# Attention over channels: the eight queries with the most keys move to ScalarE as one exponential per query and head, and TensorE sums them over the keys

## The chip, the cores and the metric

One core of one Trainium2 chip runs the whole program. The metric is device time in microseconds (us) of one execution. The five engines run in parallel, each with its own in-order instruction queue, and meet only at semaphores: TensorE (PE; its weight loads are shown as PEld), VectorE (DVE), ScalarE (ACT), GpSimd (POOL) and SyncE (SP), which issues DMAs.

## The reference, cut to what matters

The program is one transformer-like layer: a state-space recurrence, a mixture of experts, a combine step, and last an attention with a feed-forward part. The change touches the last part alone. There the attention is taken inside each token: with 16 heads of 64 channels, every channel of q is a query and every channel of k a key.

```
Q = (x @ Wq + bq).reshape(b, s, 16, 64) * 64 ** -0.5     # K, V alike, without the factor
scores = einsum("bshq,bshk->bshqk", Q, K)                # an outer product: q[i] * k[j]
scores = where(j > i, -inf, scores)                      # query i sees keys 0..i
w = softmax(scores)
attn = einsum("bshqk,bshk->bshq", w, V)
out = x + attn.reshape(b, s, 1024) @ Wo + bo + (silu(x @ Wg) * (x @ Wu)) @ Wd
```

For one token and head that is 64 x 65 / 2 = 2,080 products, exponentials and weighted values. Query 63 has 64 keys, query 0 has one.

## The kernel before, in words

4,096 tokens are cut into 32 tiles of 128, one token to a partition, and the tiles are run one after the other by one loop. Channels are kept in reverse order with the 16 heads innermost, so a query is a stretch of 16 elements. The queries are split in two units of 32: unit 0 is channels 31 to 0, unit 1 is channels 63 to 32. A tile is 24 chunks: chunks 0 to 7 are unit 0 against the near keys (31 to 0), chunks 8 to 15 are unit 1 against the near keys, a full rectangle, and chunks 16 to 23 are unit 1 against the far keys (63 to 32). The two triangles are cut by diagonals, four to a chunk; a chunk of the rectangle is four keys against all 32 queries. The chunks are 256 to 2,048 elements wide, 34,816 a tile.

Each chunk goes through five steps on four engines.

- DVE `products` (L1238, L1239 in the helper `multiply`): q times k, into one of six slots `s`. It waits until the slot's user six chunks before has been summed and multiplied.
- POOL (L1303): subtracts the maximum `m` of each query and head. The maximum is the greater of q times the largest and q times the smallest key that the query sees; POOL makes it in three instructions of 512 elements for each unit (`maxima`, L1283, L1285, L1288) from two scans of DVE.
- ACT (L1389): the exponential, with the factor 1/8 as a constant scale.
- PE `sum_den` and DVE `times_v`: PE adds the rows of the chunk into the PSUM bank `den`, by one transposing matmul against the identity for each 128 columns (`sum_rows`, L1550); DVE multiplies the chunk by v into one of four slots `pv`.
- PE `sum_num`: the same transposing sum of `pv` into the bank `num`.

Every engine's queue is written out by hand per chunk: at chunk c, PE does `sum_den(c)`, then `prepare(c)`, then `sum_num(c - 1)`, then a part of `down`. `prepare` makes the projections of K and Q for the next tile, V, and the feed-forward up-projections. They all use one PSUM bank, `work`: each fills it only after ACT has copied the one before out of it (`keep_k`, `keep_q`, `keep_v`, `keep_up`), and the tables such as `KEEP_Q0 = 19` or `SILU = 18` say after which chunk's exponential ACT does which copy. `show_k` and `show_v` put a unit's k or v into the PSUM banks `kp` and `vp` that DVE reads. DVE runs `times_v` three chunks behind `products`.

Of the kernel before, what the change touches and what calls it, by code (L numbers as in the profile page):

```python
# [1123 lines left out]
ROWS = 4  # L1124
FRONT = (ROWS - 1) * H
QL = FRONT + HALF
FULL, TAIL = ROWS * HALF, 64
LEAST = 65
HU = H // 2
NTRI = 2 * NB  # L1130
TRI_ORDER = ((0, 7, 2, 5, 4, 3, 6, 1), (0, 1, 2, 3, 4, 7, 6, 5))
NCH = 3 * NTRI
S_RING, PV_RING = 6, 4
NUP = HT // 2
USES = {"U0": 1, "K0": 2, "K1": 3, "V1": 4, "U1": 5, "U2": 6, "Q0": 7, "V0": 8, "Q1": 9}
# [6 lines left out]
def attention_and_ffn(nc, k, io, scratch):  # L1142
    with ExitStack() as ctx:
# [6 lines left out]
        q = [a.sb(f"q{i}", [P, QL]) for i in range(2)]  # L1150
        m = [a.sb(f"m{i}", [P, QL]) for i in range(2)]
        k_near, vv, fall = (a.sb(s, [P, HALF]) for s in ("k_near", "v", "fall"))
        k_far = [a.sb(f"k_far{u}", [P, HALF]) for u in range(2)]
# [8 lines left out]
        out_sb = a.sb("out_sb", [P, D])  # L1162
# [6 lines left out]
        x2_in, y_out, padded = (a.sem(s) for s in ("x2_in", "y_out", "padded"))  # L1169
        xT_in = [a.sem(f"xT_in{u}") for u in range(2)]  # L1170
# [24 lines left out]
        def work_use(t, name):  # L1195

            return t * NWORK + (5 + USES[name])

        def is_rect(c):
            return NTRI <= c < 2 * NTRI  # L1200
# [4 lines left out]
        def triangle(c):  # L1205

            start = TRI_ORDER[unit_of(c)][c % NTRI] * ROWS
            return start, (RANGE - start) * H
# [4 lines left out]
        def part(ring, c):  # L1213

            n = HALF if is_rect(c) else triangle(c)[1]
            return view(slot(ring, c)[:], [[n, ROWS], [1, n]], FULL - ROWS * n)

        def by_row(ap):

            return bass.AP(tensor=ap.tensor, offset=ap.offset, ap=[ap.ap[0], ap.ap[1], [H, RANGE], [1, H]])  # L1220

        def by_query(x, c):

            if is_rect(c):
                return view(x, [[0, ROWS], [1, HALF]], FRONT)
            return view(x, [[-H, ROWS], [1, triangle(c)[1]]], FRONT)

        def by_key(x, c):

            if is_rect(c):  # L1230
                return view(x, [[H, ROWS], [0, RANGE], [1, H]], (c - NTRI) * ROWS * H)
            start, n = triangle(c)
            return view(x, [[0, ROWS], [1, n]], start * H)
# [7 lines left out]
        with nc.Block() as block:  # L1241

            @block.sync
            def _(sp):
# [8 lines left out]
                def finish(t):  # L1253
                    wait(sp, y_ready, t)
                    settle(sp, settled)
                    sp.dma_start(x2[:], tokens(scratch["x2"])[:, bass.ds(t, 1), :].rearrange("p o d -> p (o d)")
                                 ).then_inc(x2_in, 16)
                    sp.wait_ge(y_ready, t + 1)
                    settle(sp, settled)
                    sp.dma_start(tokens(io["out"])[:, bass.ds(t, 1), :].rearrange("p o d -> p (o d)"), out_sb[:]  # L1260
                                 ).then_inc(y_out, 16)
# [12 lines left out]
            def _(pool):  # L1274
                def maxima(t, h, step):

                    n = t * 2 + h
                    turned = lambda x: view(x[:], [[-1, RANGE], [C, H]], h * RANGE + RANGE - 1)
                    rows = lambda x, at=0: view(x[:], [[H, RANGE], [1, H]], at)
# [6 lines left out]
                    else:  # L1286
                        pool.wait_ge(max_step, n * 3 + 2)
                        nc.gpsimd.tensor_tensor(m[h][:, FRONT:QL], m[h][:, FRONT:QL], fall[:], ALU.subtract  # L1288
                                                ).then_inc(max_step, 1)
# [5 lines left out]
                MAXIMA_HERE, MAXIMA_NEXT = {3: 0, 4: 1, 5: 2}, {21: 0, 22: 1, 23: 2}  # L1295
                GATED = 20

                def tile(t, u):
                    for c in range(NCH):
# [9 lines left out]
                        if c == GATED:  # L1309
                            gated(t)  # L1310

                for h in range(2):
# [4 lines left out]
                for step in range(3):  # L1317
                    maxima(0, 0, step)
                pool.wait_ge(padded, 4)
# [3 lines left out]
            def _(act):  # L1323
                def keep_k(t, u, half, source=work):
# [3 lines left out]
                    for low, dst in ((0, k_near), (RANGE, k_far[u])):  # L1328
                        ins = nc.scalar.copy(view(dst[:], [[H, RANGE], [1, HU]], half * HU),
# [3 lines left out]
                def keep_q(t, h, use, source=work):  # L1333
# [3 lines left out]
                    past = (t - 1) * NCH + (NCH if h else NTRI)  # L1337
                    wait(act, mult_done, past)
                    nc.scalar.copy(q[h][:, FRONT:QL], source[:])
                    wait(act, sub_done, past)  # L1340
                    nc.scalar.activation(m[h][:, FRONT:QL], source[:], ACT.Relu)
                    wait(act, max_step, n * 3)
                    nc.scalar.activation(fall[:], source[:], ACT.Relu, scale=-1.0).then_inc(q_out, 1)
# [11 lines left out]
                def show_k(t, u, h):  # L1355
                    act.wait_ge(k_out, t * 2 + 2)
                    wait(act, mult_done, t * NCH + h * 2 * NTRI)
                    nc.scalar.copy(kp[:], (k_far[u] if h else k_near)[:]).then_inc(kp_ready, 1)

                def show_v(t, h):  # L1360
                    act.wait_ge(v_out, t * 2 + (h + 1))
                    wait(act, pv_done, t * NCH + h * 2 * NTRI)
# [18 lines left out]
                KEEP_Q1, KEEP_V1, KEEP_Q0, KEEP_V0 = 0, 13, 19, 22  # L1381
                SUMS_PAST, SUMS_HERE = 2, 14
                KEEP_UP, SILU = {4: 0, 15: 1, 17: 2}, 18
                KEEP_K = {8: 0, 12: 1}

                def tile(t, u):
                    for c in range(NCH):
# [5 lines left out]
                        if c == KEEP_Q1:  # L1393
                            keep_q(t, 1, t * NWORK + 5)
# [13 lines left out]
                        if c == KEEP_Q0:  # L1408
                            keep_q(t + 1, 0, work_use(t, "Q0"))
                        if c == KEEP_V0:  # L1410
# [10 lines left out]
                keep_v(0, 4, source=first_v)  # L1421
                show_k(0, 0, 0)
# [4 lines left out]
            def _(dve):  # L1427
                v = nc.vector

                def products(t, c):  # L1430
# [3 lines left out]
                    if c in (0, 2 * NTRI):  # L1434
                        dve.wait_ge(kp_ready, t * 2 + (1 + c // (2 * NTRI)))
# [4 lines left out]
                def times_v(t, c):  # L1440
                    dve.wait_ge(exp_done, count(t, c))
                    if c in (0, 2 * NTRI):
                        dve.wait_ge(vp_ready, t * 2 + (1 + c // (2 * NTRI)))
# [34 lines left out]
                def output(t):  # L1478
                    dve.wait_ge(acc_done, t + 1)
                    dve.wait_ge(x2_in, 16 * (t + 1))  # L1480
                    wait(dve, y_out, 16 * t)
                    v.tensor_tensor(out_sb[:], misc[:, 0:D], x2[:], ALU.add).then_inc(y_ready, 1)

                SCAN = {8: (0, 0), 9: (0, 1), 12: (1, 0), 13: (1, 1)}
                DIVIDE_PAST, DIVIDE_HERE = {5: 0, 6: 1, 7: 2}, {20: 0, 21: 1, 22: 2}
# [3 lines left out]
                def tile(t, u):  # L1489
                    for c in range(NCH):  # L1490
# [6 lines left out]
                        elif not first(t):  # L1497
                            times_v(t - 1, NCH + c - LAG)
                        if c in SCAN:
# [21 lines left out]
            def _(pe):  # L1521
                def project(t, u, which, half, into=work):

                    pe.wait_ge(xT_in[u], 8 * (t - u) + 16)
                    cols = slice(half * HALF, half * HALF + HALF)
                    for c in range(DC):
                        nc.tensor.matmul(into[:], xT[u][:, c, :], wqkv[which][:, c, cols], start=(c == 0), stop=False)  # L1527
                    nc.tensor.matmul(into[:], part_rows[:], bias[:, which, cols], start=False, stop=True
# [13 lines left out]
                def sum_rows(dst, ring, c):  # L1542

                    buf, n = slot(ring, c), HALF if is_rect(c) else triangle(c)[1]
                    for x in range(ROWS):
                        late = 0 if is_rect(c) else x * H
                        for b in range(math.ceil((n - late) / P)):
                            at = FULL - (ROWS - x) * n + late + b * P
                            wide = max(LEAST, min(P, n - late - b * P))
                            ins = nc.tensor.matmul(dst[0:wide, b * P:(b + 1) * P], buf[:, at:at + wide], k.ident[:],  # L1550
                                                   start=(c in (0, NTRI) and x == 0 and b == 0), stop=False,
                                                   is_transpose=True, skip_group_check=True)
                    return ins

# [32 lines left out]
                DOWN_HERE, DOWN_PAST = {20: 0, 21: 1, 22: 2, 23: 3}, {2: 4, 5: 5, 8: 6}  # L1587
# [160 lines left out]
```

## Time and profile before

| | |
|---|---|
| median of 2 runs | 3773.43 us (3771.79 to 3775.06) |
| profiled execution | 3769.08 us |
| its span, first to last instruction | 3767.3 us |
| mean granted TensorE clock | 0.973 of full speed |
| busy over the span | PE 93%, POOL 88%, DVE 86%, PEld 81%, ACT 48% |
| attention tiles | from about 914 us to the end |
| chain that ended last | POOL 30%, issue 23%, PE 15%, DVE 6%, ACT 1% |
| costliest group | POOL L1303, 768 instructions, 2506.5 us |

The busy shares are averages over a program of several stages. In the last three quarters of the span the page's slices are all alike: that is the loop over the 32 tiles. "Issue" in the chain is time in which an engine waited for nothing that the profile shows.

### The profile page before, as it was taken

The numbers are of one execution on the slowest core, as the hardware profiler recorded it, in microseconds if no ns is written. First come the engines' busy times: TensorE is split into PE (matmuls) and PEld (weight loads), VectorE is DVE, ScalarE is ACT, GpSimd is POOL, SyncE is SP. The second block draws the span as 40 slices with busy tenths as digits, with TensorE's granted clock in tenths as the row PEclk, the third lists the DMA queues.
The fourth block names the chain that finished last, engine by engine and source line by source line (L and its number), as shares of the span: only waits on it lengthen the run. The fifth ranks groups of instructions, "written<-read, shape, count | busy, mean of one in ns | idle before, by whom it ended". The sixth has DMA issues, their size and how long they took to land.

```text
span 3767.3 us, 72478 instructions
## 1 busy us (share of the span) xinstructions
PE 3493.9 (93%) x25868; PEld 3070.0 (81%) x26061; DVE 3233.5 (86%) x3516; ACT 1808.7 (48%) x2391; POOL 3307.3 (88%) x1507
## 2 busy tenths in 40 slices
PE   3684999977999999999999999999999999999999
PEld 2342988866888888888888888888888888888888
DVE  8422777666999999999999999999999999999998
ACT  1110443444555555555555555555555555555554
POOL 1677555524999999999999999999999999999998
PEclk7797999998999999999999999999999999999999
DMA  9523566684000000000000000000000000000000
GB/s 377 180 102 110 179 205 204 211 315 165 4 5 5 5 7 5 5 8 5 5 6 6 5 5 5 5 5 5 5 5 6 7 5 8 5 5 6 5 5 5
DMA packets 110620, 209.17 MB, mean 56 GB/s; under 512 B 16609, under 2 KB 77281, under 8 KB 110305
## 3 DMA queue, kind: packets, MB, share of 16 engines
q1 hardware_dynamic: 84192, 140.90, 11.4%
q0 software_dynamic: 21504, 59.93, 4.3%
q8 instruction: 191, 3.13, 0.3%
q10 hardware_dynamic: 4608, 4.20, 0.3%
q14 instruction: 125, 1.02, 0.1%
HBM read 183.34 MB, written 107.74 MB: 77 GB/s over the span
## 4 chain that ended last, share of the span: by engine, by line
POOL 30%; issue 23%; PE 15%; DVE 6%; ACT 1%; another core or an unknown queue 0%; POOLq 0%; DVEq 0%; ACTq 0%
POOL at_s L1303 26%; PE at_num L1550 6%; PE at_den L1550 5%; DVE at_s L1238 3%; PE at_work L1527 2%; DVE at_pv L1238 2%; POOL at_m L1288 2%; PE at_work L1537 1%; POOL at_fall L1285 1%; POOL at_m L1283 1%; PE at_misc L1576 1%; DVE at_k_low L1457 1%; PE at_misc L1582 1%; DVE at_k_top L1454 0%; DVE at_pv L1239 0%
## 5 line engine op out<-in xcount | busy, mean ns | idle before, releaser
L1303 POOL TENSOR_TENSOR at_s<-at_s,at_m 128x2048 f32<-128x2048 f32 (+7 forms) x768 | 2506.5, 3307 | 5.2 <-POOL at_m L1288 4.7
L1389 ACT ACTIVATE at_s<-at_s 128x2048 f32<-128x2048 f32 (+7 forms) x768 | 1085.7, 1419 | 1085.1 <-POOL at_s L1303 1084.5
L1550 PE MATMUL at_num<-k_ident,at_pv 128*128 128x128 f32 (+2 forms) x9216 | 1135.9, 273 | 64.9 <-DVE at_pv L1238 54.5
L1550 PE MATMUL at_den<-k_ident,at_s 128*128 128x128 f32 (+2 forms) x9216 | 1138.6, 273 | 18.2 <-ACT at_s L1389 15.9
L1550 PEld LDWEIGHTS at_num<-k_ident,at_pv 128*128 128x128 f32 (+2 forms) x9216 | 1025.8, 139 | 150.2 <-DVE at_pv L1238 84.1
L1550 PEld LDWEIGHTS at_den<-k_ident,at_s 128*128 128x128 f32 (+2 forms) x9216 | 1029.8, 139 | 55.8 <-ACT at_s L1389 19.1
L1239 DVE TENSOR_TENSOR at_pv<-at_s,at_vp 128x2048 f32<-128x2048 f32 (+7 forms) x512 | 690.2, 1348 | 121.9 <-PE at_num L1550 63.2
L1239 DVE TENSOR_TENSOR at_s<-at_q,at_kp 128x2048 f32<-128x2048 f32 (+7 forms) x512 | 689.4, 1347 | 27.7 <-PE at_den L1550 24.3
L1238 DVE TENSOR_TENSOR at_pv<-at_s,at_vp 128x2048 f32<-128x2048 f32 x256 | 583.9, 2281 | 0.0
L1238 DVE TENSOR_TENSOR at_s<-at_q,at_kp 128x2048 f32<-128x2048 f32 x256 | 581.2, 2270 | 0.0
L706 POOL DMA_INDIRECT picked<-moe_yo,moe_row x256 | 245.8, 960 | 172.0 <-ACT moe_yo L761 84.0
L1527 PE MATMUL at_work<-k_region,at_xT 128*128 128x512 f32 x776 | 367.6, 596 | 7.2 <-DMA at_xT<-xT 7.2
L142 POOL DMA_INDIRECT slot_x<-e_xn,e_slot x192 | 190.9, 994 | 136.6 <-DMA slot_x<-k_region 75.4
L728 PE MATMUL moe_gu<-moe_xT,c_w 128*128 128x128 f32 x2048 | 278.4, 279 | 5.7 <-DVE moe_xT L850 5.7
L728 PEld LDWEIGHTS moe_gu<-moe_xT,c_w 128*128 128x128 f32 x2048 | 250.3, 193 | 17.3 <-DVE moe_xT L850 13.2
L1527 PEld LDWEIGHTS at_work<-k_region,at_xT 128*128 128x128 f32 x776 | 133.3, 192 | 101.7 <-issue 93.8
L767 ACT ACTIVATE moe_gate<-moe_gu 128x128 f32<-128x128 f32 x256 | 71.1, 278 | 270.7 <-PE moe_gu L728 270.7
L1537 PE MATMUL at_work<-at_xT,k_region 128*128 128x128 f32 x1536 | 187.2, 275 | 0.0
L1537 PEld LDWEIGHTS at_work<-at_xT,k_region 128*128 128x128 f32 x1536 | 179.1, 192 | 0.0
L844 DVE TENSOR_TENSOR moe_hid<-moe_gate,moe_gu 128x128 f32<-128x128 f32 x256 | 73.1, 286 | 104.9 <-ACT moe_gate L767 99.5
L735 PE MATMUL moe_yp<-c_w,moe_hid 128*128 128x256 f32 x512 | 153.3, 381 | 0.3 <-DVE moe_hid L844 0.3
L850 DVE COPY moe_xT<-moe_tr 128x256 f32<-128x256 f32 x256 | 107.1, 418 | 47.3 <-PE moe_tr L719 45.9
(248 smaller groups left out, 3007.0 us busy)
## 6 DMA issues: line engine op xcount, KB each, us to landing
c_w<-experts SPq DMA_DIRECT2D x256, 384.0 KB
slot_x<-k_region SPq DMA_DIRECT2D x16, 2144.0 KB, 25.0
moe_x<-slot_x SPq DMA_DIRECT2D x256, 134.0 KB
cmb_y<-picked SPq DMA_DIRECT2D x32, 768.0 KB, 9.1
at_xT<-xT SPq DMA_DIRECT2D x33, 128.0 KB, 2.0
e_x<-u SPq DMA_DIRECT2D x4, 1024.0 KB, 9.7
picked<-moe_yo,moe_row POOLq DMA_INDIRECT x256
xT<-cmb_xT ACTq DMA_DIRECT2D x32, 128.0 KB, 6.2
```

The source lines that it names most:

```text
L142: nc.gpsimd.indirect_dma_start(scratch["slot_x"], bass.IndirectOffsetOnAxis(ap=k.slot[:, n, j:j + 1], axis=0), k.xn[:, n, :], None).then_i ...
L706: pool.indirect_dma_start(scratch["picked"], bass.IndirectOffsetOnAxis(ap=row[i % 2][:, j:j + 1], axis=0), yo[j][:], None).then_inc(y_out[ ...
L728: ins = nc.tensor.matmul(gu[j % 2][:, s, :], w[j][:, (2 * s + c) * P:(2 * s + c + 1) * P], xT[j][:, c, :], start=(c == 0), stop=(c == DC - 1))
L735: nc.tensor.matmul(yp[j % 2][:], hid[j][:], w[j][:, 2 * D:3 * D], start=True, stop=True).then_inc(y_done, 1)
L850: nc.vector.tensor_copy(xT[j][:], tr[j % 2][:]).then_inc(xT_ready, 1)
L1238: return nc.vector.tensor_tensor(by_row(out), by_row(other), keys, ALU.mult)
L1239: return nc.vector.tensor_tensor(out, other, keys, ALU.mult)
L1303: nc.gpsimd.tensor_tensor(part(s_slot, c), part(s_slot, c), by_query(m[unit_of(c)][:], c), ALU.subtract).then_inc(sub_done, 1)
L1389: nc.scalar.activation(part(s_slot, c), part(s_slot, c), ACT.Exp, scale=C ** -0.5).then_inc(exp_done, 1)
L1527: nc.tensor.matmul(into[:], xT[u][:, c, :], wqkv[which][:, c, cols], start=(c == 0), stop=False)
L1537: ins = nc.tensor.matmul(work[:, (2 * s + h) * P:(2 * s + h + 1) * P], w[:, c, tile * P:(tile + 1) * P], xT[u][:, c, :], start=(c == 0), s ...
L1550: ins = nc.tensor.matmul(dst[0:wide, b * P:(b + 1) * P], buf[:, at:at + wide], k.ident[:], start=(c in (0, NTRI) and x == 0 and b == 0), s ...
```

## The change: what it does

The eight queries with the most keys (channels 63 to 56, with 64 to 57 keys) leave the chunks. The maxima of these 128 pairs of query and head are made apart (`keep_top`, `top_maxima`). For each pair ACT runs one exponential over all the keys that the query sees, with q/8 as its scale and minus the maximum as its bias, both read from a column of one element per partition (`top_rows`): 128 instructions a tile, eleven after each of chunks 0 to 10 and seven after chunk 11. They read the keys of one head, 16 elements apart, from `k_all`, and write a column of `top_p`, 128 elements apart. `top_p` holds 64 keys x 128 pairs, once. PE then sums `top_p` over the keys by 64 transposing matmuls (`sum_top_den`, chunks 12 and 13), DVE multiplies it by v in place in eight instructions of 1,024 elements (`top_times_v`, chunks 15 to 20), and PE sums it again by 64 more (`sum_top_num`, near keys at chunk 18, far keys at chunk 21). After that `top_summed` tells ACT that `top_p` is free.

The other chunks shrink. Unit 1 has 24 queries instead of 32 in the rectangle and in its triangle, and the triangles are cut into groups of three to five diagonals. A tile is still 24 chunks, with 27,344 elements in place of 34,816; chunks 1 to 12 hold 15,728 of them. The transposing matmuls of the chunks go from 288 to 224 for `den` and from 288 to 224 for `num`. The projection of unit 1's queries is made in two parts, 128 columns (`QA`) and 384, and the steps of `prepare`, the copies of ACT, `silu`, `divide` and `down` take other chunks. The stored result is added into `x2` itself, and SP loads `x2` for the next tile after that store has landed.

```diff
+TOP = BLK
+SHORT = RANGE - TOP
+AW = TOP * H
+TRI = (((0, 3), (27, 5), (3, 3), (22, 5), (6, 3), (17, 5), (9, 4), (13, 4)),
+       ((0, 3), (3, 3), (6, 3), (9, 3), (12, 3), (21, 3), (18, 3), (15, 3)))
+QW = (HALF, REST)
+FULL, TAIL = 3 * HALF, 64
...
+        k_all = [a.sb(f"k_all{u}", [P, C * H]) for u in range(2)]
+        top_p = a.sb("top_p", [P, C * AW])
...
@@ SP
                 def finish(t):
-                    wait(sp, y_ready, t)
-                    settle(sp, settled)
+                    wait(sp, y_out, 16 * t)
                     sp.dma_start(x2[:], tokens(scratch["x2"])[:, bass.ds(t, 1), :].rearrange("p o d -> p (o d)")
...
@@ POOL
+                def top_maxima(t):
...
+                    pool.wait_ge(top_kept, t + 1)
+                    nc.gpsimd.tensor_tensor(rows(top_m), turned(k_top), rows(top_m), ALU.mult).then_inc(top_step, 1)
+                    nc.gpsimd.tensor_tensor(rows(top_fall), turned(k_low), rows(top_fall), ALU.mult).then_inc(top_step, 1)
+                    pool.wait_ge(top_step, t * 3 + 2)
+                    nc.gpsimd.tensor_tensor(top_m[:], top_fall[:], top_m[:], ALU.subtract).then_inc(top_step, 1)
...
-                MAXIMA_HERE, MAXIMA_NEXT = {3: 0, 4: 1, 5: 2}, {21: 0, 22: 1, 23: 2}
-                GATED = 20
+                MAXIMA_HERE, MAXIMA_NEXT = {3: 0, 4: 1, 5: 2}, {18: 0, 19: 1, 20: 2}
+                GATED, TOP_MAXIMA = 18, 21
...
+                nc.gpsimd.memset(top_p[:], 0.0).then_inc(zeroed, 1)
@@ ACT
+                def keep_top(t, use):
+                    act.wait_ge(work_done, use)
+                    wait(act, top_step, t * 3)
+                    nc.scalar.activation(top_q[:], work[:, 0:AW], ACT.Copy, scale=C ** -0.5)
+                    nc.scalar.activation(top_m[:], work[:, 0:AW], ACT.Relu, scale=C ** -0.5)
+                    nc.scalar.activation(top_fall[:], work[:, 0:AW], ACT.Relu, scale=-C ** -0.5).then_inc(top_kept, 1)
+
+                def top_rows(t, u, low, high):
+                    if low == 0:
+                        act.wait_ge(top_step, t * 3 + 3)
+                        act.wait_ge(k_out, t * 2 + 2)
+                        wait(act, top_summed, t)
+                    for n in range(low, high):
+                        row, head = divmod(n, H)
+                        ins = nc.scalar.activation(view(top_p[:], [[AW, C - row]], row * AW + n),
+                                                   view(k_all[u][:], [[H, C - row]], row * H + head), ACT.Exp,
+                                                   bias=top_m[:, n:n + 1], scale=top_q[:, n:n + 1])
+                    if high == AW:
+                        ins.then_inc(rows_done, 1)
...
                 def show_v(t, h):
...
+                    if h:
+                        act.wait_ge(top_pv, t * 2 * NGROUP + NGROUP)
...
-                KEEP_Q1, KEEP_V1, KEEP_Q0, KEEP_V0 = 0, 13, 19, 22
+                KEEP_Q1, KEEP_V1, KEEP_Q0, KEEP_TOP, KEEP_V0 = 0, 13, 16, 17, 18
-                KEEP_UP, SILU = {4: 0, 15: 1, 17: 2}, 18
+                KEEP_UP, SILU = {4: 0, 14: 1, 15: 2}, 16
+                ROWS_AT = [11] * 11 + [7]
...
+                        if c < len(ROWS_AT):
+                            top_rows(t, u, sum(ROWS_AT[:c]), sum(ROWS_AT[:c + 1]))
@@ DVE
+                def top_times_v(t, far, g):
+                    dve.wait_ge(top_den_done, t * 2 + (2 if far else 1))
+                    at = (0 if far else RANGE) * AW + g * GROUP * H
+                    piece = view(top_p[:], [[AW, RANGE], [H, GROUP], [1, H]], at)
+                    v.tensor_tensor(piece, piece, view(vp[:], [[H, RANGE], [0, GROUP], [1, H]]), ALU.mult
+                                    ).then_inc(top_pv, 1)
...
+                TOP_V = {15: ((0, 0),), 16: ((0, 1),), 17: ((0, 2),), 18: ((0, 3),),
+                         19: ((1, 0), (1, 1)), 20: ((1, 2), (1, 3))}
@@ PE
+                def sum_top_den(t, far):
+                    pe.wait_ge(rows_done, t + 1)
+                    for key in range(0 if far else RANGE, RANGE if far else C):
+                        ins = nc.tensor.matmul(den[1][:, 0:P], top_p[:, key * AW:(key + 1) * AW], k.ident[:],
+                                               start=False, stop=False, is_transpose=True, skip_group_check=True)
+                    ins.then_inc(top_den_done, 1)
+
+                def sum_top_num(t, far):
+                    pe.wait_ge(top_pv, t * 2 * NGROUP + (NGROUP + NGROUP * far))
...
+                    if far:
+                        ins.then_inc(top_summed, 1)
...
-                DOWN_HERE, DOWN_PAST = {20: 0, 21: 1, 22: 2, 23: 3}, {2: 4, 5: 5, 8: 6}
+                DOWN_HERE, DOWN_PAST = {18: 0, 19: 1, 20: 2}, {1: 3, 2: 4, 5: 5, 8: 6}
+                TOP_NUM, TOP_DEN = {18: 0, 21: 1}, {12: 0, 13: 1}
```

In the new order of PE, `prepare` makes V at chunk 12, the up-projections at 13 and 14, Q of unit 0 at 15, `QA` at 16, V of the next tile at 17 and the other 384 columns at 18; `sum_top_num` and `sum_top_den` stand behind `sum_num(c - 1)` at their chunks.

## Rows read from the trace of the kernel before

**Rows 1.** Stages: us, then busy us of each engine (x instructions), granted PE clock, DMA.
```profile
2000.00:2500.00 500.00, 486.69 (x3824) 440.01 (x3856) 477.44 (x330) 271.06 (x277) 498.69 (x170) 1.00 0.02 6
```
**Rows 2.** One line of the kernel, L1293, once a tile: ns min/median/max, first and last start.
```profile
L1293 POOL TENSOR_TENSOR at_hid<-at_hid,at_gu_sb x32: 1824/1862/1968, 992.4 to 3740.7; 128x768 f32<-128x768 f32 x32
```
**Rows 3.** Waits from 1500 to 3500 us: us in total, times, longest us.
```profile
ACT at_s L1389 <- POOL at_s L1303: 749.8, 366, 5.1
...
PEld at_num L1550 <- DVE at_pv L1238: 62.0, 67, 1.3
```
**Rows 4.** Groups by shape, 1500 to 3500 us, POOL: busy us, mean ns, idle before.
```profile
L1303 POOL TENSOR_TENSOR at_s<-at_s,at_m 128x2048 f32<-128x2048 f32 x224 | 1017.0, 4591 | 3.8 <-POOL at_m L1288 3.5 <-DVE at_s L1239 0.3
...
L1283 POOL TENSOR_TENSOR at_m<-at_k_top,at_m 128x512 f32<-128x512 f32 x46 | 72.0, 1566 | 2.2
...
L1288 POOL TENSOR_TENSOR at_m<-at_m,at_fall 128x512 f32<-128x512 f32 x45 | 58.1, 1292 | 0.0
...
L1303 POOL TENSOR_TENSOR at_s<-at_s,at_m 128x256 f32<-128x256 f32 x46 | 34.4, 749 | 0.0
```
**Rows 5.** The same view, DVE.
```profile
L1238 DVE TENSOR_TENSOR at_pv<-at_s,at_vp 128x2048 f32<-128x2048 f32 x180 | 410.5, 2281 | 0.0
...
L1239 DVE TENSOR_TENSOR at_pv<-at_s,at_vp 128x256 f32<-128x256 f32 x46 | 19.1, 415 | 0.0
```
**Rows 6.** The same view, ACT.
```profile
L1389 ACT ACTIVATE at_s<-at_s 128x2048 f32<-128x2048 f32 x225 | 431.6, 1918 | 516.9 <-POOL at_s L1303 516.7
...
L1389 ACT ACTIVATE at_s<-at_s 128x256 f32<-128x256 f32 x46 | 19.6, 426 | 0.0
```
**Rows 7.** Timeline of ACT: start us, us, instruction; five of one tile.
```profile
2517.68 0.43 ACT L1389 ACTIVATE at_s<-at_s 128x256 f32<-128x256 f32 x1
2517.99 0.61 ACT L1363 COPY at_vp<-at_v 128x512 f32<-128x512 f32 x1
2518.54 1.49 ACT L1389 ACTIVATE at_s<-at_s 128x1536 f32<-128x1536 f32 x1
2519.93 0.58 ACT L1370 ACTIVATE at_log_den<-at_den 128x512 f32<-128x512 f32 x1
...
2521.08 0.83 ACT L1389 ACTIVATE at_s<-at_s 128x768 f32<-128x768 f32 x1
```
**Rows 8.** Timeline of ACT in the combine step: twenty instructions, merged into one row.
```profile
786.79 5.95 ACT L1053 ACTIVATE cmb_diag<-k_ident,e_choice_w 128x128 f32<-128x128 f32 x20 [3.51 <-PEq L689]
```
**Rows 9.** The line of these, L1053: ns min/median/max, first and last start.
```profile
L1053 ACT ACTIVATE cmb_diag<-k_ident,e_choice_w x160: 384/386/403, 786.8 to 879.1; 128x128 f32<-128x128 f32 x160
```
**Rows 10.** Timeline of PE's weight loads in one tile: start us, us, loads merged.
```profile
2543.22 0.30 PEld L1527 LDWEIGHTS at_work<-k_region,at_xT 128*128 128x128 f32 x2
...
2545.04 1.88 PEld L1550 LDWEIGHTS at_num<-k_ident,at_pv 128*128 128x128 f32 x16 [0.33 <-issue]
2546.90 0.73 PEld L1582 LDWEIGHTS at_misc<-k_region,at_attnT 128*128 128x128 f32 x4
2547.66 1.88 PEld L1550 LDWEIGHTS at_den<-k_ident,at_s 128*128 128x128 f32 x16
2549.51 1.78 PEld L1550 LDWEIGHTS at_num<-k_ident,at_pv 128*128 128x128 f32 x16
2551.26 1.78 PEld L1550 LDWEIGHTS at_den<-k_ident,at_s 128*128 128x128 f32 x16
...
2571.46 1.86 PEld L1537 LDWEIGHTS at_work<-at_xT,k_region 128*128 128x128 f32 x16
```
**Rows 11.** The same view in the first tile, around a long wait.
```profile
945.65 2.51 PEld L1550 LDWEIGHTS at_den<-k_ident,at_s 128*128 128x128 f32 x16 [2.58 <-ACT at_s L1389]
948.14 0.55 PEld L1527 LDWEIGHTS at_work<-k_region,at_xT 128*128 128x128 f32 x2
...
950.86 1.88 PEld L1550 LDWEIGHTS at_num<-k_ident,at_pv 128*128 128x128 f32 x16 [0.33 <-issue]
```
**Rows 12.** Stages, as in rows 1, of that stretch.
```profile
943.00:951.00 8.00, 5.68 (x24) 3.88 (x23) 8.00 (x5) 4.36 (x4) 8.00 (x3) 0.79 0.01 2
```

More of the change, by code:

```diff
@@ L1169, in attention_and_ffn @@
         x2_in, y_out, padded = (a.sem(s) for s in ("x2_in", "y_out", "padded"))
+        top_kept, top_step, rows_done, top_den_done, top_pv, top_summed = (
+            a.sem(s) for s in ("top_kept", "top_step", "rows_done", "top_den", "top_pv", "top_summed"))
         xT_in = [a.sem(f"xT_in{u}") for u in range(2)]
@@ L1310, in tile @@
                             gated(t)
+                        if c == TOP_MAXIMA:
+                            top_maxima(t + 1)
+                nc.gpsimd.memset(top_p[:], 0.0).then_inc(zeroed, 1)
                 for h in range(2):
@@ L1318, in _ @@
                     maxima(0, 0, step)
+                top_maxima(0)
                 pool.wait_ge(padded, 4)
@@ L1327, in keep_k @@
                     wait(act, kp_ready, t * 2 - 1)
-                    for low, dst in ((0, k_near), (RANGE, k_far[u])):
-                        ins = nc.scalar.copy(view(dst[:], [[H, RANGE], [1, HU]], half * HU),
+                    for low, at in ((0, HALF), (RANGE, 0)):
+                        ins = nc.scalar.copy(view(k_all[u][:], [[H, RANGE], [1, HU]], at + half * HU),
                                              view(source[:], [[-1, RANGE], [C, HU]], low + RANGE - 1))
@@ L1393, in tile @@
                         if c == KEEP_Q1:
[L1394 removed]
+                            keep_q(t, 1, t * NWORK + 6)
                         if c == SUMS_PAST and not first(t):
@@ L1421, in _ @@
                 keep_v(0, 4, source=first_v)
+                keep_top(0, 5)
+                act.wait_ge(zeroed, 1)
                 show_k(0, 0, 0)
@@ L1498, in tile @@
                             times_v(t - 1, NCH + c - LAG)
+                        for far, g in TOP_V.get(c, ()):
+                            top_times_v(t, far, g)
                         if c in SCAN:
@@ L1521, in _, with project @@
             def _(pe):
-                def project(t, u, which, half, into=work):
+                def project(t, u, which, half, into=work, low=0, high=HALF):
                     pe.wait_ge(xT_in[u], 8 * (t - u) + 16)
-                    cols = slice(half * HALF, half * HALF + HALF)
+                    cols, out = slice(half * HALF + low, half * HALF + high), into[:, 0:high - low]
                     for c in range(DC):
-                        nc.tensor.matmul(into[:], xT[u][:, c, :], wqkv[which][:, c, cols], start=(c == 0), stop=False)
-                    nc.tensor.matmul(into[:], part_rows[:], bias[:, which, cols], start=False, stop=True
+                        nc.tensor.matmul(out, xT[u][:, c, :], wqkv[which][:, c, cols], start=(c == 0), stop=False)
+                    nc.tensor.matmul(out, part_rows[:], bias[:, which, cols], start=False, stop=True
                                      ).then_inc(work_done, 1)
@@ L1553, in sum_rows @@
                     return ins
+                def sum_top_den(t, far):
[6 more added lines that the diff above has]
+                    pe.wait_ge(top_pv, t * 2 * NGROUP + (NGROUP + NGROUP * far))
+                    for key in range(0 if far else RANGE, RANGE if far else C):
+                        ins = nc.tensor.matmul(num[1][:, 0:P], top_p[:, key * AW:(key + 1) * AW], k.ident[:],
+                                               start=False, stop=False, is_transpose=True, skip_group_check=True)
+                    if far:
+                        ins.then_inc(top_summed, 1)
                 def sum_den(t, c):
@@ L1640, in _ @@
                 pe.wait_ge(v_out, 1)
-                pe.wait_ge(zeroed, PV_RING + S_RING)
+                pe.wait_ge(zeroed, PV_RING + S_RING + 1)
                 tile_loop(pe, tile)
                 sum_num(NT - 1, NCH - 1)
-                for step in range(4, 7):
+                for step in range(3, 7):
                     down(NT - 1, step)
```

138 lines of the change are left out of this document (81 added, 57 removed).

## The prediction, on record before the kernel ran

> **What bounds the kernel now.** I read the busy time by stage first. In the attention loop POOL is busy 498.69 of 500 us, PE 486.69, DVE 477.44 and ACT only 271.06, at the full TensorE clock, granted 1.00 [rows 1]. One instruction that stands once in each tile gives the period: from the first to the last of 32 starts it is (3740.7 - 992.4) / 31 = 88.65 us a tile [rows 2]; so PE is busy 86.3 us a tile, DVE 84.6, ACT 48.1. The waits say who is late: ACT waits 749.8 us in 2,000 for POOL's subtraction, PE's loads 62.0 us for DVE [rows 3]. POOL sets the pace, with PE 2.3 us a tile behind it. The span of 3767.3 us is 1.8 us short of the execution's 3769.08, and that is 4.4 us below the median 3773.43; I sum against the execution and add the 4.4 at the end.
>
> **The engines' totals after the change.** POOL: its chunks cost (4591 - 749) / 1792 = 2.14 ns an element and 0.20 us each [rows 4], so 27,344 elements in 24 chunks are 63.4 us; the maxima, 2 x 1.57 + 1.29 = 4.4 us for 512 columns [rows 4], are needed for 512 + 384 + 128 columns, 8.8 us; with the gating of 1.9 [rows 2] POOL comes to 74 us. DVE: 1.04 ns an element [rows 5] on 7,472 fewer elements, twice, is -15.6 us; eight top products of 1,024 elements at 1.22 us are +9.7; 79 us. PE: 64 transposing matmuls fewer for each of the two sums, 64 more for each: 576 before and after. Splitting a projection adds one bias step and its loads, which I put at 0.3 us: 86.6 us. ACT: the exponentials cost (1918 - 426) / 1792 = 0.833 ns an element [rows 6], -6.2 us, and 128 small ones come in.
>
> **The price of a small exponential** decides, and no row shows it: 60.5 elements on average, two operands that are columns of one element per partition, strided in and out. An exponential without such operands starts its successor after 2517.99 - 2517.68 = 0.31 us at 256 elements [rows 7], 0.31 - 0.213 = 0.097 us above its elements. Twenty instructions with one such operand (a scale from `choice_w`) take 5.95 us, each lasting 0.386 [rows 8, 9]: one start every (5.95 - 0.386) / 19 = 0.293 us, 0.186 above their 128 elements. The first operand so costs 0.089 us. The second costs between nothing and as much again; I take as much again, its only near row being the first one's. That is 0.050 + 0.097 + 2 x 0.089 = 0.325 us, 128 of them 41.6 us a tile. ACT's total is 48.1 - 6.2 + 41.6, and some 0.5 for `keep_top`: 84 us. By these totals every engine stays under today's period, and PE's 86.6 would set the new one.
>
> The Trainium skill, "ScalarE: Activation LUTs", section "What ACT_TABLE_LOAD costs", states about 93 ns for each pointer operand, and as much overlap between neighbours; by it the exponential would be 0.33 us and the forecast some 20 us later. For the first operand the trace agrees, with 89 ns; for two no row here shows it.
>
> **The loop that the totals hide.** `top_p` exists once. ACT writes it behind chunks 0 to 11; PE reads it from chunk 12 on and gives it back (`top_summed`) after the far sum of chunk 21; ACT's first top row of the next tile waits for that, and behind it in ACT's queue stand the exponentials of chunks 1 to 23. Chunk 12 of PE needs chunk 12's exponential, which ACT issues after all 128 rows. So one tile costs ACT's stretch plus PE's stretch, one after the other, however early everything else is.
>
> ACT's stretch, first row to the exponential of chunk 12: 128 rows, 41.6; the twelve exponentials of chunks 1 to 12, 15,728 elements, 13.1, and 12 x 0.11 between them (1.39 us from start to start at 1,536 elements [rows 7]), 1.3; `show_v` 0.55 and the two steps of `reciprocal` 1.15 [rows 7]; `keep_up`, a copy like `show_v`'s, 0.55, and `keep_k`, two of 256 elements, 0.6. Sum 58.9 us.
>
> PE's stretch, chunk 12 to the far sum in chunk 21: 89 transposes for `den`, 98 for `num`, 128 for the top queries. Thirty-two take 2551.26 - 2547.66 = 3.60 us [rows 10], 0.1125 each: 315 are 35.4. Four projections at 2545.04 - 2543.22 = 1.82 [rows 10] and the split's 0.3: 7.6. Two up-projections at 1.8 [rows 10]: 3.6. Three steps of `down` at 0.76 [rows 10]: 2.3. Sum 48.9 us.
>
> **Other waits in the loop.** PE's handoffs through `work` are late only if ACT is. `silu` with its table loads now lies between Q's projection and its copy, but PE has 24 transposes (2.7 us) there. DVE waits at chunk 15 for `top_den_done`; behind it stand `products` 16 and later and POOL's and ACT's chunks after them, and PE needs their sums later still: by the prices above DVE has the near products some 22 us into PE's stretch, PE asks for them at 35; the far ones at 35, asked for at 44. ACT's `show_v` now waits for the near products, at 22 us, with `keep_top` behind it, which PE asks for at 30. POOL runs `gated`, the maxima and `top_maxima` closer together; its chunk 0 of the next tile comes at about 44 us of 49, its exponential and `keep_q` 3 us later, just ahead of `top_summed`. If it came later it would add what is missing, at most a few us. I cost these at nothing. While ACT is slow, PE has 37 us of work in 59, so it waits some 2 us in each of chunks 5 to 11. In the first tile such a wait, 2.58 us, was followed by sixteen loads in 2.51 us and a projection of 950.86 - 948.14 = 2.72 [rows 11], with a mean granted clock of 0.79 over 8 us, so partly at 1.2 GHz [rows 12]: 0.7 + 0.9 = 1.6 us lost. Where such a spell reaches into chunk 12 it is on the path: between 0 and 1.6 us, and I take half, 0.8.
>
> SP's store from `x2` and the load that waits for it have a whole tile to land; the next `xT` load stays behind the same store as before, so nothing. Ahead of the loop come a memset of 8,192 elements on POOL, at the price of a subtraction 18 us at most and partly under POOL's own wait, and one `keep_top`: between 0 and 20 us once, I take 3.
>
> **Sum.** 58.9 + 48.9 + 0.8 = 108.6 us a tile, 19.95 more than 88.65; 32 tiles are 638; 3769.1 + 638 + 3 = 4410, and the 4.4: **4415 us**, 17% more.
>
> **The rivals.**
>
> 1. *The second operand is free* (both columns fetched together). A row is 0.236 us, a tile 97.2, the time 4050. For it: nothing shows the second's cost. Against: nothing shows two fetched at once, and the first was not hidden.
>
> 2. *Strided elements cost extra.* POOL's multiplication that reads `k_top` 64 elements apart takes 1566 ns against 1292 for its neighbour without stride [rows 4]: 0.53 ns an element for one strided operand. Two of them in a row of 60.5 add 0.065 us, 8.3 a tile: 116.9, and 4680. For it: that row. Against: another engine, and another operation. The Trainium skill speaks against the change here: "Advanced Engine Details and Errata", section "SBUF Cachelines", states that walking to another 16-byte line with each element loses speed, and both walks of a row do; the POOL row agrees with it as far as one row can.
>
> 3. *Not slower:* the small exponentials run at the price of one without column operands, 0.147 us, 18.8 a tile. ACT's stretch is then 36 us, the loop 85.8 with the 0.8, less than PE's 86.6, and PE sets a period of about 86.7: 3710. It turns at (88.65 - 48.9 - 0.8 - 17.3) / 128 = 0.17 us an exponential. Against it: the rows of one operand lie above that, 0.236 at this size. That would also be the outcome if ACT's rows ran a tile ahead, which one `top_p` forbids.
>
> **How the numbers follow.** Of no change a measurement of this kernel can tell about 2%, 75 us. Chances: the forecast 0.64, the free operand 0.11, the strides 0.14, not slower 0.09, and 0.02 for a still longer loop (more half-clock spells, late chunks of POOL). The forecast's own range is 4320 to 4510, from 0.31 to 0.34 us a row and the two ends of the clock's term. To hold 8 in 10 I take in the strides and what lies between the free operand's 4050 and the forecast only in part: **4230 to 4700**. Rival 3's 3710 is at the edge of 2%: faster by over 2% 0.03, within 2% 0.06, slower 0.91.
>
> **What would show it.** The 4,096 rows' group on ACT with a mean of some 0.41 us, starting every 0.325 us (0.24 free, 0.39 strided). A period of 108 us, read from the line of `gated`. POOL's and DVE's busy shares in the loop falling to about 70%, PE's to about 80%, with PE's idle time before `den`, released by ACT's exponential. ACT waiting in each tile after chunk 0's exponential and `keep_q` for PE's top sum: if ACT never waits there, the loop isn't closed and the sum is wrong. A period near 87 us with PE over 98% busy would make it wrong altogether; a period between 95 and 100 would mean the price of a row.

## The result, and the profile after

4610.18 us median (4610.16 to 4610.21, 2 runs) against 3773.43: 1.2228 times the time before, 95% interval 1.2208 to 1.2247. Slower, as forecast, and inside the range of 4230 to 4700; but it is 195 us above the forecast of 4415, outside that forecast's own range (4320 to 4510), and only 70 us below the 4680 of rival 2, the strided elements, which had a chance of 0.14.

In the loop DVE and POOL now have less to do and PE issues as many transposing matmuls as before, and all three stand idle more; ACT is busier. The stage view (us, then busy us of PE, PEld, DVE, ACT, POOL with their instructions, granted PE clock, DMA) and the once-a-tile line that answer to [rows 1, 2]:

```profile
2000.00:2500.00 500.00, 409.63 (x2982) 363.20 (x3005) 343.79 (x289) 387.47 (x781) 313.90 (x143) 0.95 0.02 5
```
```profile
L1329 POOL TENSOR_TENSOR at_hid<-at_hid,at_gu_sb x32: 1817/1835/1853, 1015.7 to 4577.9; 128x768 f32<-128x768 f32 x32
```

The period is (4577.9 - 1015.7) / 31 = 114.9 us a tile, where it was 88.65. No engine is near full: PE 82%, ACT 77%, DVE 69%, POOL 63%. That fits a loop that passes from engine to engine. The waits that answer to [rows 3] (2000 to 4000 us, some 17 tiles: us, times, longest) say the same:

```profile
POOL at_s L1339 <- DVE at_s L1263: 402.9, 141, 8.5
PEld at_den L1635 <- ACT at_s L1456: 376.9, 186, 3.4
...
DVE at_top_p L1525 <- PE at_den L1645: 119.9, 18, 6.8
...
ACT at_top_p L1402 <- PE at_num L1653: 18.1, 17, 1.1
```

POOL, which set the pace, now waits; PE waits for ACT's exponentials; and once in every tile ACT's first top row waits 1.1 us for PE's top sum. That last wait is small, and it is the important one: ACT reached `top_p` 1.1 us before PE gave it back, and started 0.1 us after that in every tile. The chain that ended last (pieces in order of time: start, us, what) follows it through one tile:

```profile
2412.08 3.51 PE at_num L1653 x32
2416.48 3.59 ACT at_top_p L1402 x9
2421.31 3.97 ACT at_top_p L1402 x10
2425.28 1.25 ACT at_s L1456
...
2476.12 1.48 ACT at_s L1456
2477.64 2.82 PE at_den L1635 x12
...
2486.70 3.49 PE at_den L1645 x32
...
2517.28 3.49 PE at_num L1653 x32
...
2527.19 3.51 PE at_num L1653 x32
2531.60 3.59 ACT at_top_p L1402 x9
```

From the far sum of one tile to the far sum of the next the chain is ACT's rows and exponentials, then PE's sums and projections, and no piece of another engine. The stage view of these two stretches:

```profile
2415.70:2481.60 65.90, 45.64 (x297) 39.75 (x298) 43.90 (x32) 65.87 (x147) 42.12 (x17) 0.90 0.01 3
2481.60:2530.60 49.00, 48.84 (x387) 44.31 (x389) 35.11 (x35) 23.62 (x36) 30.91 (x19) 1.00 0.02 7
```

In the first ACT is busy 65.87 of 65.90 us, in the second PE 48.84 of 49.00. They follow each other; that is the whole 114.9. The timeline of ACT at the start of a tile, which answers to [rows 7], and the page's line of the rows (busy us, mean ns) show the rows' price:

```profile
2415.69 4.38 ACT L1402 ACTIVATE at_top_p<-at_k_all,at_top_m,at_top_q 128x64 f32<-128x64 f32 x11 [1.09 <-PE at_num L1653]
2419.97 0.52 ACT L1456 ACTIVATE at_s<-at_s 128x400 f32<-128x400 f32 x1
```
```profile
L1402 ACT ACTIVATE at_top_p<-at_k_all,at_top_m,at_top_q 128x64 f32<-128x64 f32 (+7 forms) x4096 | 1606.1, 489 | 33.3 <-PE at_num L1653 33.3
```

Eleven rows in 4.38 us, each lasting 0.49 with the start of the next inside it: one every (4.38 - 0.49) / 10 = 0.389 us, where I had 0.325.

### The profile page after: what moved, and what is told of

It reads as the page before. It is cut to its first block, busy times and chain, and to the rows that moved or that the text cites. A ratio compares the mean times of both kernels' runs of the same rounds, so it can differ in the third digit from the quotient of the medians.

```text
span 4608.4 us, 77628 instructions
## 1 busy us (share of the span) xinstructions
PE 3766.9 (82%) x26065; PEld 3267.7 (71%) x26226; DVE 3065.2 (67%) x3772; ACT 3137.3 (68%) x6586; POOL 2830.8 (61%) x1607
## 4 chain that ended last, share of the span: by engine, by line
ACT 38%; PE 35%; issue 7%; POOL 0%; DVE 0%; another core or an unknown queue 0%; ACTq 0%; POOLq 0%
ACT at_top_p L1402 33%; PE at_num L1635 8%; PE at_den L1635 8%; PE at_work L1611 5%; PE at_num L1653 5%; PE at_den L1645 5%; ACT at_s L1456 5%; PE at_work L1621 2%; PE at_misc L1679 2%; ACT at_log_den L1436 0%; ACT at_k_all L1369 0%; PE at_work L1612 0%; ACT at_inv L1438 0%; ACTq L50 0%
## 5 line engine op out<-in xcount | busy, mean ns | idle before, releaser
L1339 POOL TENSOR_TENSOR at_s<-at_s,at_m 128x1536 f32<-128x1536 f32 (+13 forms) x768 | 2006.9, 2622 | 1180.3 <-DVE at_s L1263 737.5
L1402 ACT ACTIVATE at_top_p<-at_k_all,at_top_m,at_top_q 128x64 f32<-128x64 f32 (+7 forms) x4096 | 1606.1, 489 | 33.3 <-PE at_num L1653 33.3
L1635 PE MATMUL at_den<-k_ident,at_s 128*128 128x128 f32 (+4 forms) x7168 | 1024.3, 294 | 602.6 <-ACT at_s L1456 598.7
L1635 PEld LDWEIGHTS at_den<-k_ident,at_s 128*128 128x128 f32 (+4 forms) x7168 | 871.9, 150 | 719.7 <-ACT at_s L1456 688.4
L1456 ACT ACTIVATE at_s<-at_s 128x1536 f32<-128x1536 f32 (+13 forms) x768 | 886.6, 1154 | 266.7 <-POOL at_s L1339 266.7
L1635 PE MATMUL at_num<-k_ident,at_pv 128*128 128x128 f32 (+4 forms) x7168 | 983.1, 287 | 61.0 <-DVE at_pv L1264 52.5
L1264 DVE TENSOR_TENSOR at_pv<-at_s,at_vp 128x576 f32<-128x576 f32 (+13 forms) x512 | 578.9, 1131 | 605.6 <-ACT at_s L1456 482.3
L1635 PEld LDWEIGHTS at_num<-k_ident,at_pv 128*128 128x128 f32 (+4 forms) x7168 | 879.2, 148 | 133.6 <-issue 118.2
L1264 DVE TENSOR_TENSOR at_s<-at_q,at_kp 128x576 f32<-128x576 f32 (+13 forms) x512 | 577.3, 1128 | 106.7 <-PE at_den L1635 92.9
L1263 DVE TENSOR_TENSOR at_pv<-at_s,at_vp 128x1536 f32<-128x1536 f32 x256 | 448.5, 1752 | 234.0 <-ACT at_s L1456 234.0
L728 PEld LDWEIGHTS moe_gu<-moe_xT,c_w 128*128 128x128 f32 x2048 | 251.2, 193 | 17.3 <-DVE moe_xT L850 13.1
```

What stands on the lines that cost most here:

```text
L728: ins = nc.tensor.matmul(gu[j % 2][:, s, :], w[j][:, (2 * s + c) * P:(2 * s + c + 1) * P], xT[j][:, c, :], start=(c == 0), stop=(c == DC - 1))
L1263: return nc.vector.tensor_tensor(by_row(out), by_row(other), keys, ALU.mult)
L1264: return nc.vector.tensor_tensor(out, other, keys, ALU.mult)
L1339: nc.gpsimd.tensor_tensor(part(s_slot, c), part(s_slot, c), by_query(m[unit_of(c)][:], c), ALU.subtract).then_inc(sub_done, 1)
L1402: ins = nc.scalar.activation(view(top_p[:], [[AW, C - row]], row * AW + n), view(k_all[u][:], [[H, C - row]], row * H + head), ACT.Exp, bi ...
L1456: nc.scalar.activation(part(s_slot, c), part(s_slot, c), ACT.Exp, scale=C ** -0.5).then_inc(exp_done, 1)
```

## The experiments

In what follows ACT's stretch runs from the first top row to the end of chunk 12's exponential, the rest from there to the next tile's first row; both are means over 27 tiles of the trace.

| kernel | ACT's stretch | the rest | period | median us |
|---|---|---|---|---|
| the change | 65.9 | 49.0 | 114.9 | 4610.18 |
| e1_mix | 54.9 | 49.1 | 104.0 | 4260.01 (one run) |
| e2_unit | 59.1 | 49.2 | 108.3 | 4398.69 |
| e3_early | 66.9 | 43.7 | 110.5 | 4469.9 |
| e5_major_early | 60.0 | 44.3 | 104.4 | 4275.17 |
| e6_half_one | 59.6 | 49.4 | 109.1 | 4418.05 |
| e7_half_two | 59.6 | 46.2 | 105.8 | 4316.19 |

**e1_mix: what a row's parts cost.**

```diff
-                        ins = nc.scalar.activation(view(top_p[:], [[AW, C - row]], row * AW + n),
-                                                   view(k_all[u][:], [[H, C - row]], row * H + head), ACT.Exp,
-                                                   bias=top_m[:, n:n + 1], scale=top_q[:, n:n + 1])
+                        out = view(top_p[:], [[1, C - row]], n * C) if write_unit else view(top_p[:], [[AW, C - row]], row * AW + n)
+                        keys = view(k_all[u][:], [[1, C - row]], n) if read_unit else view(k_all[u][:], [[H, C - row]], row * H + head)
+                        extra = {}
+                        if "b" in columns:
+                            extra["bias"] = top_zero[:, n:n + 1]
+                        extra["scale"] = top_zero[:, n:n + 1] if "s" in columns else 0.0
+                        ins = nc.scalar.activation(out, keys, ACT.Exp, **extra)
...
+                MIX = ((0, 0, "sb"), (1, 0, "sb"), (0, 1, "sb"), (1, 1, "sb"), (0, 0, "s"), (0, 0, "b"),
+                       (0, 0, ""), (1, 1, "s"), (1, 1, "b"), (1, 1, ""), (0, 0, "sb"), (0, 0, "sb"))
```

> The 128 small exponentials of a tile take nine forms, by the chunk behind which they stand; scale and bias columns hold zeros, so the top queries' weights are wrong, and one semaphore orders each chunk's rows behind the last. Chunks 0, 10, 11 as in the changed kernel; 1: keys read side by side; 2: written side by side; 3: both; 4: scale column only, bias constant; 5: bias column only; 6: neither column; 7, 8, 9: read and written side by side with the scale column only, the bias column only, neither. Theory (column operands at 0.09 us each, and the strides by the element): start to start 0.385 us as it is, 0.35 to 0.36 with one walk side by side, 0.325 with both, 0.295 with one column and strides, 0.21 with none and strides, 0.235 with one column side by side, 0.147 with none. Rival (strides are free, a row with columns has a fixed price of 0.38 to 0.39): chunks 1 to 3 like chunk 0. Rival (the second column is free and the strides cost 0.15): one column and strides 0.385, both columns side by side 0.235.

The timeline of ACT in one tile of it, the rows behind chunks 0 to 10 (start, us for all eleven):

```profile
2481.77 4.38 ACT L1412 ACTIVATE at_top_p<-at_k_all,at_top_zero 128x64 f32<-128x64 f32 x11 [1.09 <-PE at_num L1665]
2487.00 3.81 ACT L1412 ACTIVATE at_top_p<-at_k_all,at_top_zero 128x64 f32<-128x64 f32 x11
2493.05 4.34 ACT L1412 ACTIVATE at_top_p<-at_k_all,at_top_zero 128x63 f32<-128x63 f32 x11
2498.19 3.73 ACT L1412 ACTIVATE at_top_p<-at_k_all,at_top_zero 128x62 f32<-128x62 f32 x11
2503.50 3.30 ACT L1412 ACTIVATE at_top_p<-at_k_all,at_top_zero 128x62 f32<-128x62 f32 x11
2507.80 3.29 ACT L1412 ACTIVATE at_top_p<-at_k_all,at_top_zero 128x61 f32<-128x61 f32 x11
2512.30 2.27 ACT L1412 ACTIVATE at_top_p<-at_k_all 128x60 f32<-128x60 f32 x11
2515.63 2.69 ACT L1412 ACTIVATE at_top_p<-at_k_all,at_top_zero 128x60 f32<-128x60 f32 x11
2520.11 2.70 ACT L1412 ACTIVATE at_top_p<-at_k_all,at_top_zero 128x59 f32<-128x59 f32 x11
2524.07 1.66 ACT L1412 ACTIVATE at_top_p<-at_k_all 128x58 f32<-128x58 f32 x11
2527.00 4.26 ACT L1412 ACTIVATE at_top_p<-at_k_all,at_top_zero 128x58 f32<-128x58 f32 x11
```

Medians from start to start over the 32 tiles, worked out from the starts in the trace, in us: as it is 0.389; keys side by side 0.332; written side by side 0.386; both 0.330; strided with the scale alone 0.290, with the bias alone 0.290, with neither 0.199; side by side with the scale alone 0.235, with the bias alone 0.235, with neither 0.141. So a column operand costs 0.09 us, scale or bias, the second as much as the first; the strided read costs 0.05 to 0.06 a row; the strided write costs nothing that can be seen (0.386 with one key fewer than 0.389). The theory's numbers hold but for one: it split the strides' cost between read and write, and all of it lies in the read. Both rivals fall. The Trainium skill's "ScalarE: Activation LUTs", section "What ACT_TABLE_LOAD costs", puts a pointer operand at 93 ns. The rows of 0.141, 0.235 and 0.330 us have mostly 58, 59 and 62 keys; less 0.833 ns a key they are 0.093, 0.186 and 0.278, so both steps are about 93 ns: the trace agrees, now for the second operand too.

**e2_unit: the row's price in the loop.** All rows take the form of e1's chunk 3.

```diff
-                        ins = nc.scalar.activation(view(top_p[:], [[AW, C - row]], row * AW + n),
-                                                   view(k_all[u][:], [[H, C - row]], row * H + head), ACT.Exp,
-                                                   bias=top_m[:, n:n + 1], scale=top_q[:, n:n + 1])
+                        ins = nc.scalar.activation(view(top_p[:], [[1, C - row]], n * C),
+                                                   view(k_all[u][:], [[1, C - row]], n), ACT.Exp,
+                                                   bias=top_zero[:, n:n + 1], scale=top_zero[:, n:n + 1])
```

> All 128 rows of a tile read and write side by side, with both columns (holding zeros; the top queries' weights are wrong). Theory (strides cost 0.06 us a row, and the tile is ACT's stretch plus PE's): rows 0.325 us, 7.6 us a tile less, a period of 107 us and 4365 us in all. Rival (strides free): 4610. Rival (no loop, the period comes from clock or handoffs of PE): 4610, whatever the rows cost.

Measured 4398.69 us; 108.3 us a tile. ACT's stretch lost 6.8 us, 0.053 a row, and the rest was 49.2. The theory had 7.6 us and 4365, 34 us too low, because it put the strides at 0.06 a row. Both rivals said 4610 and fall. A row at the forecast's price gives about the forecast's time: this kernel took 16 us less than the 4415.

**e3_early: PE's stretch shortened, no work removed.**

```diff
-USES = {"U0": 1, "K0": 2, "K1": 3, "V1": 4, "U1": 5, "U2": 6, "Q0": 7, "QA": 8, "V0": 9, "Q1": 10}
+USES = {"U0": 1, "U1": 2, "U2": 3, "K0": 4, "K1": 5, "V1": 6, "Q0": 7, "QA": 8, "V0": 9, "Q1": 10}
...
-                KEEP_UP, SILU = {4: 0, 14: 1, 15: 2}, 16
+                KEEP_UP, SILU = {2: 0, 3: 1, 4: 2}, 16
...
-                DOWN_HERE, DOWN_PAST = {18: 0, 19: 1, 20: 2}, {1: 3, 2: 4, 5: 5, 8: 6}
+                DOWN_HERE, DOWN_PAST = {22: 0, 23: 1}, {0: 2, 1: 3, 2: 4, 5: 5, 8: 6}
```

> The same work, in another order on PE: up-projections 1 and 2 move from chunks 13 and 14 to chunks 2 and 3 (the first from 2 to 1), and down steps 0 to 2 from chunks 18 to 20 to 22, 23 and the next tile's 0; their copies on ACT move with them. Theory (loop): PE's stretch loses 3.6 + 2.3 us, ACT's gains two copies of 0.5, a period of 110 us and 4455 us, though no engine has less to do. Rival (an engine's total or PE's clock sets the period): 4610 within 20.

4469.9 us, ratio to before 1.1858 (1.1838 to 1.1878); 110.5 us a tile. ACT's stretch gained 1.0 us, the rest lost 5.3 of the 5.9 that were moved. Every engine issues what it issued, and 140 us are gone: the totals don't set the period. Nor does PE's clock: it was granted at 1.00 in the rest in both kernels. The missing 0.6 us shows a second path. No top row waits for PE any more; the first starts 1.2 us after the far top sum has ended, right behind chunk 0's exponential and the copies of `keep_q`. DVE's timeline of one tile, with ACT's first rows, shows what they wait for:

```profile
2431.38 1.22 DVE L1525 TENSOR_TENSOR at_top_p<-at_top_p,at_vp 128x1024 f32<-128x1024 f32 x1 [6.57 <-PE at_den L1645]
...
2458.76 1.75 DVE L1264 TENSOR_TENSOR at_s<-at_q,at_kp 128x1536 f32<-128x1536 f32 x1 [0.23 <-DVE at_pv L1264]
```
```profile
2466.61 4.38 ACT L1402 ACTIVATE at_top_p<-at_k_all,at_top_m,at_top_q 128x64 f32<-128x64 f32 x11
```

From PE's near top sum (chunk 12) DVE runs with 0.23 us of gaps to chunk 0's products, and POOL's subtraction, ACT's exponential and `keep_q` follow. This path, too, contains ACT's stretch and the start of PE's. In the change itself ACT was ready for the rows 1.1 us before `top_p` came back; here it is ready about 1.1 us after.

**e4_no_rows: the loop made short.**

```diff
-                    for n in range(low, high):
-                        row, head = divmod(n, H)
...
+                    if low % 33 == 0:
+                        piece = top_p[:, low // 33 * 2048:(low // 33 + 1) * 2048]
+                        ins = nc.scalar.activation(piece, piece, ACT.Exp, scale=0.0)
```

> The 128 exponentials of a tile are replaced by four of 2,048 elements that write ones into top_p (so the top queries' weights are left out); all waits stay. Theory: ACT's stretch is 16.7 + 7.2 us, the loop 73, so it no longer sets the period, and PE's total does: 86.6 to 88 us a tile, 3710 to 3760 us. Rival (PE's handoffs or DVE's waits for the top sums set it): over 95 us a tile, over 3980.

3752.39 us, 0.9956 of before (0.994 to 0.9972). Its once-a-tile line and a stage of it:

```profile
L1329 POOL TENSOR_TENSOR at_hid<-at_hid,at_gu_sb x32: 1820/1837/1849, 985.0 to 3718.1; 128x768 f32<-128x768 f32 x32
```
```profile
2000.00:3000.00 1000.00, 981.91 (x7804) 891.88 (x7803) 886.38 (x758) 555.87 (x644) 830.30 (x383) 1.00 0.02 6
```

A period of 88.2 us with PE busy 98.2%, 86.6 us a tile. With the rows nearly free the change is worth 0.4%, and the rival (over 95 us) falls: POOL was relieved by 17%, and PE, which does as many transposing matmuls as before, takes its place at once.

**e5_major_early: both repairs at once.** The order of e3, and the keys kept head by head (`keep_k`, which writes them so in one copy instead of two, is left out here):

```diff
-                                                   view(k_all[u][:], [[H, C - row]], row * H + head), ACT.Exp,
+                                                   view(k_all[u][:], [[1, C - row]], head * C + row), ACT.Exp,
...
-                    at = 0 if h else HALF
-                    nc.scalar.copy(kp[:], k_all[u][:, at:at + HALF]).then_inc(kp_ready, 1)
+                    nc.scalar.copy(view(kp[:], [[H, RANGE], [1, H]]),
+                                   view(k_all[u][:], [[1, RANGE], [C, H]], 0 if h else RANGE)).then_inc(kp_ready, 1)
```

> The whole computation, with the order of e3 and the keys kept head by head, so that a row reads its keys side by side (kp is then filled by a strided copy). Theory (the reads' stride costs 0.055 us a row, and the two stretches add up): from e3's 110.5 us a tile minus 7.0, 103.5, and 4245 us. Rival (the stretches overlap, so that only the longer counts): less than 60 us saved against e3's 4470.

4275.17 us, 1.134 of before (1.1307 to 1.1372), the best of the kernels here that compute everything, and still slower than before. It saves 195 us against e3, where the rival allowed 60. ACT's stretch lost 6.8 us, the rest gained 0.6, and the time is 30 us above the 4245 that I expected. As in e3 no row waits for PE: the first starts 1.7 us after the far top sum has ended, 0.5 us later than in e3; on the path through DVE, chunk 0's products now wait 0.7 us for `kp`, whose copy has become a strided one (1.08 us in place of 0.60).

**e6_half_one and e7_half_two: one buffer or two.** The edit of e7 against e6:

```diff
-        top_p = a.sb("top_p", [P, RANGE * AW])
+        top_p = [a.sb(f"top_p{i}", [P, RANGE * AW]) for i in range(2)]
...
-                        wait(act, top_summed, t)
+                        wait(act, top_summed, t - 1)
```

> 128 rows of 32 keys instead of 57 to 64, columns of zeros, one top_p of half the size; PE sums each of the 32 keys twice, so it issues as many matmuls as before, and DVE's top products are half as long (half the keys are left out, and the weights are wrong). Theory: a row is 0.187 + 0.094 + 32 x 1.76 ns = 0.335 us, ACT's stretch 16.7 + 42.9, PE's 49.0, a period of 108.6 us and 4410 us. Rival (rows have a fixed price): 4610.

> The kernel of e6 with two such top_p by turns, so that ACT's rows wait for the tile before the last. Theory: the loop through top_p is gone, but chunk 0's subtraction on POOL and the copies of ACT before the first row come only about 2 us before top_summed came; the period falls by 1 to 3 us, 106 us and 4325 us, and a second buffer alone would not have saved the change. Rival (top_p's one copy was all that held the tile): the engines' totals are left, ACT 85 and PE 88 us, a period below 95 and under 3990 us.

4418.05 and 4316.19 us; 109.1 and 105.8 us a tile, both near what the theory had, and both rivals fall. Rows of 32 keys start every 0.333 us, so the price has the part by the element and the fixed part that e1 gave. The second buffer takes only 3.2 us from the rest. In e7 no row waits for PE's top sum any more: the first starts 3.2 us before that sum has ended. Two long waits of e7 (2000 to 4000 us, 19 tiles):

```profile
DVE at_top_p L1528 <- PE at_den L1648: 135.8, 19, 7.2
POOL at_m L1309 <- ACT at_fall L1387: 117.8, 19, 6.2
```

DVE stands 7 us a tile at chunk 15 for PE's top sum with `products` behind it, and POOL 6 us for the copy of Q. The timelines of one tile say which comes last here:

```profile
2585.14 0.59 ACT L1419 COPY at_gu_sb<-at_work 128x512 f32<-128x512 f32 x1 [5.91 <-PE at_work L1624]
...
2591.23 0.60 ACT L1387 ACTIVATE at_fall<-at_work 128x512 f32<-128x512 f32 x1
```
```profile
2591.91 1.54 POOL L1309 TENSOR_TENSOR at_m<-at_k_top,at_m 128x512 f32<-128x512 f32 x1 [6.20 <-ACT at_fall L1387]
```
```profile
2593.34 1.35 DVE L1265 TENSOR_TENSOR at_pv<-at_s,at_vp 128x1152 f32<-128x1152 f32 x1 [6.27 <-ACT at_s L1459]
```

DVE, after its wait at chunk 15, waits again, 6.27 us, and goes on 0.1 us after ACT's `show_v` has ended, so its first wait is not what is late here. From the copy of Q on POOL works up to chunk 0's subtraction with 0.2 us of gaps, and DVE ends chunk 0's products within 0.1 us of POOL getting there. Both hang on ACT, which had waited 5.91 us for PE's last up-projection and then did `silu`, the copy of Q and `show_v`. So a second loop, again through ACT's rows and the start of PE's stretch, lay 3 us under the first.

## Why the prediction was right, and where it was off

- *The loop.* Right. By engine totals the change looked like a small gain; by the one copy of `top_p` it was ACT's stretch plus PE's. e2, e3 and e5 move one stretch or both and the period follows; e7 shows that the release of `top_p` held the tile, but by 3 us only. The copy of `top_p` is thus not the only thing that puts the two stretches one after the other: in e3, e5 and e7 no row waits for it, which in the changed kernel would have been the prediction's sign of a wrong sum, and the period is still within 1 us of the expected sum of the two stretches in e3 and e5 and 3 us under it in e7, because the queues of DVE, POOL and ACT join the same stretches. Rival 3 names one `top_p` as what forbids rows a tile ahead; e7 shows that a second one alone doesn't give them.
- *PE's stretch.* Forecast 48.9 us, measured 49.0, from counts and rows of before alone. Forecast PE total 86.6, and e4 has 86.6.
- *ACT's stretch without the rows.* Forecast 17.3; 65.9 less 128 x 0.382, the rows' mean from start to start, is 17.0.
- *The row.* This is the term that was mis-sized: 0.325 us against 0.376 to 0.389 by length. The two column operands were right (0.097 + 2 x 0.089 fixed, measured 0.28 with 0.09 each). The strided read was left out of the forecast and made a rival, with 0.065 us priced from one POOL instruction [rows 4]; it costs 0.05 to 0.06. That is the right rival for half the right reason: it priced two walks at 0.53 ns an element each, and the read alone costs about 0.9 and the write nothing. The row's 0.057 too little, times 128 and 32 tiles, is 233 us; the forecast's other terms were about 40 us too high. The wide range held because it took this rival in; the forecast's own did not.
- *The clock.* Forecast 0.8 us a tile on the path; the stage view shows the granted clock at 1.00 in all of PE's stretch, and the 1.2 GHz spells in ACT's stretch (0.90), where PE waits anyway. Nothing on the path: 26 us too much. Off the path the forecast was too low: PE is busy 45.64 us in ACT's stretch, where it counted 37 at full clock.
- *The work around the loop.* In the changed kernel DVE's and POOL's new waits cost nothing, as forecast, with 1.1 us to spare; they are what is late next (e3, e5, e7).
- *Not slower* would have needed 0.17 us a row. e1 has 0.141 for a row without columns or strides, so the mechanism exists, but its premises don't hold here; and e4 shows that even then 0.4% is all there is.

## What to carry to other kernels

When work moves to an idle engine, add up the engines' totals and then follow every buffer that exists once: where the reader starts only when the writer is done, writer's stretch plus reader's stretch is a floor under the period that no total shows. Before doubling such a buffer, look for the next path that joins the same stretches: here the second buffer gained 3 us a tile. A long run of tiny instructions is priced by their fixed parts (here 0.28 us of 0.33 without the strided read): count the operands that come from memory columns and the strided reads before the elements. And before relieving the busiest engine, look how far below it the next one stands; here it was 2 us.

## What the runs showed of the hardware that was not expected

On ACT a strided read from SBUF (64 bytes from element to element) takes about 1.75 ns an element in place of 0.83 [rows 6]: rows of 64 keys start every 0.389 us in the change, rows of 32 every 0.333 in e6. A strided write (512 bytes) takes no more than a plain one: 0.332 us for 64 keys in e5, which writes so, and in e2, which doesn't. The Trainium skill's "Advanced Engine Details and Errata", section "SBUF Cachelines", has a penalty for walking from line to line without a size or a direction; the trace agrees for the read, and for the write it shows no penalty.
